# Expert choice in six parts spread over the blocks, and a bank map of its own for the last block

## The reference

```python
x = x + linear_attn(layernorm(x))        # 16 heads of 32, phi = elu + 1, causal running sums
# expert layer on the new x, 8 experts:
probs = softmax(layernorm(x) @ gate_w.T) # [16384, 8]
top2_w, top2_idx = top_k(probs, 2)       # ties go to the lower index
counts = bincount(top2_idx, length=8)
keep = counts <= int(1.25 * 16384 / 8)   # 2560: an expert with more tokens is dropped whole
out = x + sum over the two chosen experts of w * keep * ffn_e(layernorm(x))
```

## Time and profile before

| | us |
|---|---|
| median of 3 runs (2035.15 to 2038.97) | 2037.31 |
| profiled execution | 2035.86 |
| its span, first to last instruction | 2033.8 |
| PE busy in the span | 1972.9 (97%) |
| DVE busy | 1510.8 (74%) |
| POOL busy | 902.3 (44%) |
| ACT busy | 736.0 (36%) |
| load of 128 rows for the residual, issue to landing | 2.7 |
| store of them | 2.0 |

### The profile page before, as it was taken

One profiled execution on the slowest core, in us unless ns is written; L12 is line 12 of the kernel. 1 busy time (PEld: TensorE's weight loads), 2 busy tenths in 40 slices (PEclk: granted clock), 3 DMA queues, 4 the chain that ended last, 5 costly groups with the idle time before them and its releaser, 6 DMA issues.

```text
span 2033.8 us, 60809 instructions
## 1 busy us (share of the span) xinstructions
PE 1972.9 (97%) x25924; PEld 1736.7 (85%) x25924; DVE 1510.8 (74%) x3181; ACT 736.0 (36%) x1415; POOL 902.3 (44%) x987
## 2 busy tenths in 40 slices
PE   6899999999999999999999999999999999999985
PEld 5788888888888888888888888888888888888874
DVE  5677777777777777777777777777777777777767
ACT  3333343333343333343333333333343333333321
POOL 3454534554533554533554533554533554543521
PEclk8999999999999999999999999999999999999997
DMA  5221222221222221222221222221222221222110
GB/s 176 72 86 43 89 90 74 95 85 50 83 90 74 95 85 49 88 86 74 95 85 52 82 89 74 95 85 53 85 85 74 95 85 54 84 84 74 54 33 32
DMA packets 87388, 159.26 MB, mean 78 GB/s; under 512 B 15312, under 2 KB 15312, under 8 KB 87120
## 3 DMA queue, kind: packets, MB, share of 16 engines
q1 hardware_dynamic: 84720, 154.83, 22.5%
q10 hardware_dynamic: 2400, 0.55, 0.1%
HBM read 121.66 MB, written 33.68 MB: 76 GB/s over the span
## 4 chain that ended last, share of the span: by engine, by line
PE 91%; DVE 6%; POOL 1%; issue 1%; ACT 1%; DMA 0%; SPq 0%; POOLq 0%; DVEq 0%
PE ring L585 35%; PE ring L599 33%; PE num_ps L685 6%; PE ring L650 6%; PE num_ps L673 3%; PE ring L661 3%; PE num_ps L697 2%; DVE s_mask L847 2%; DVE den L1067 1%; PE ring L622 1%; PE ring L635 1%; DVE rden L1074 1%; DVE v_tok L877 1%; DVE o_lo L1063 1%; ACT o_hi L816 0%
## 5 line engine op out<-in xcount | busy, mean ns | idle before, releaser
L1136 POOL TENSOR_TENSOR k_sum<-k_sum,q_raw 128x512 f32<-128x512 f32 x128 | 164.6, 1286 | 588.8 <-DVE q_raw L858 588.8
L765 ACT ACTIVATE e_tmp<-ring,bias_n 128x512 f32<-128x512 f32 x256 | 176.0, 687 | 402.1 <-PE ring L585 402.1
L847 DVE TENSOR_TENSOR s_mask<-ring,causal 128x512 f32<-128x512 f32 x512 | 315.0, 678 | 0.0
L599 PE MATMUL ring<-wv_hi,xt_hi 128*128 128x260 f32 x1024 | 301.8, 295 | 3.1 <-DVE gate_x L879 2.3
L599 PE MATMUL ring<-wo_hi,o_hi 128*128 128x260 f32 x1024 | 290.7, 284 | 4.3 <-DVE o_lo L1063 3.5
L599 PE MATMUL ring<-wo_hi,o_lo 128*128 128x260 f32 x1024 | 293.0, 286 | 0.0
L599 PE MATMUL ring<-wo_lo,o_hi 128*128 128x260 f32 x1024 | 291.3, 284 | 0.0
L599 PE MATMUL ring<-wv_hi,xt_lo 128*128 128x260 f32 x1024 | 290.1, 283 | 0.0
L599 PE MATMUL ring<-wv_lo,xt_hi 128*128 128x260 f32 x1024 | 289.7, 283 | 0.0
L858 DVE SCALAR_TENSOR_TENSOR k_t<-ring,bias,e_tmp 128x512 f32<-128x512 f32 x128 | 96.1, 751 | 211.9 <-ACT e_tmp L767 209.0
L585 PE MATMUL ring<-xt_hi,wk_hi 128*128 128x512 f32 x512 | 215.3, 421 | 6.9 <-DVE wk_lo L310 5.6
(11 more groups left out here) (140 smaller groups left out, 4195.0 us busy)
## 6 DMA issues: line engine op xcount, KB each, us to landing
x_tok<-in_x SPq DMA_DIRECT2D x128, 256.0 KB, 3.7
res<-in_x SPq DMA_DIRECT2D x128, 256.0 KB, 2.7
out<-res SPq DMA_DIRECT2D x128, 256.0 KB, 2.0
x_in<-in_x_t SPq DMA_DIRECT2D x124, 256.0 KB, 4.5
x_rows<-moments_rows SPq DMA_DIRECT2D x31, 512.0 KB, 3.7
k_t<-in_wk_t SPq DMA_DIRECT2D x1, 1024.0 KB, 9.1
q_raw<-in_wq_t SPq DMA_DIRECT2D x1, 1024.0 KB, 11.3
v_tok<-in_wv_t SPq DMA_DIRECT2D x1, 1024.0 KB, 13.4
```

The source lines that it names most:

```text
L599: mm = pe.matmul(bank[:, 0:HW], rows[a](k), w[b][:, k, h, :], start=n == 0, stop=n == 3 * KD - 1)
L765: act.activation(e_tmp[:, m], bank, ACT.Relu, bias=bias_n[:, m, g:g + 1], scale=-1.0).then_inc(phi_relu.handle, 1)
L847: dve.tensor_tensor(s_mask[:, j], ring[:, BANK[u]].rearrange("p (g t) -> p g t", g=KD), repeat(causal, KD), ALU.mult).then_inc(free[BANK[u ...
L1136: pool.tensor_tensor(k_sum[:, g], k_sum[:, g], q_raw[:, g], ALU.mult).then_inc(prod.handle, 1)
```

## The change

1. `PARTS` has six parts instead of two: blocks 0-7, 8-15, 16-23, 24-28, 29-30 and 31, with 256, 256, 256, 160, 64 and 32 elements a partition. Parts 0 to 3 run within steady blocks (the last within block 30): steps 0 and 1 at the end of tile 3 of one block, and in the next block the exponential on ACT after `k_tok` of tile 0, steps 2 to 5 ahead of DVE's second projection chunks in tile 0, 6 to 12 at the end of tile 0, 13 to 16 in tile 1 and 17 to 18 in tile 2 ahead of `o_lo`. Part 4 is spread over the four tiles of block 31; its last two steps follow the last logits; part 5 comes at the end.
2. The steps work in place in two buffers, `den` and `rden_high` (which the denominators use in tile 2); ACT waits for the part to be over before it writes `den`. One step goes (product and sum are one `scalar_tensor_tensor`), and the count stands ahead of the weights: 19 steps.
3. Block 31 has a map of its own, `BANK_ALONE`: scores j in bank j, T in bank 4, O in banks 5 (first half) and 4 (second half). T(c+1) no longer shares a bank with scores.
4. The logits of block 31 go from POOL to DVE (`last_logits`), but for the power, which stays on POOL (`last_rstd`) with the copies of the moments.
5. PE sums the counts with six matmuls, one a part, each after its own part's count.

```diff
+BANK_ALONE = {**{("S", (c, j)): j for c in range(1, TPB) for j in range(HPG)},
+              **{("T", c): HPG for c in range(TPB)},
+              **{("O", (c, h)): HPG + 1 - h for c in range(TPB) for h in range(2)}}
...
+    def alone(self):
+
+        return self.parts == ("attn",)
+
+    def bank(self, u):
+
+        return BANK_ALONE[u] if self.alone() else BANK[u]
...
-CHOOSE_STEPS, SHIFTED = 20, 2
+CHOOSE_STEPS, SHIFTED, Z_LINKS = 19, 2, 6
...
-    half = KD * BT // 2
-    scratch = [buf.rearrange("p k t -> p (k t)")[:, h * half:(h + 1) * half] for buf in (x_in, k_sum)
-               for h in range(2)]
-    top_scratch = e_tmp[:, 0]
-    assert n_blocks * TPB * E <= half and n_blocks * TPB <= BT
-    PARTS = [(0, (n_blocks - 1) * TPB), ((n_blocks - 1) * TPB, n_blocks * TPB)]
+    z_rstd, z_last = sem("z_rstd"), sem("z_last")
+    scratch = (den, rden_high.bitcast(F32))
+    PARTS = [(0, 8), (8, 16), (16, 24), (24, n_blocks - 3), (n_blocks - 3, n_blocks - 1), (n_blocks - 1, n_blocks)]
+
+    def part_begun(t):
+
+        return [m for m, (a, b) in enumerate(PARTS[:4]) if b == t]
 
     def exponential(act, m):
         a, b = PARTS[m]
         act.wait_ge(chosen.handle, m * CHOOSE_STEPS + SHIFTED)
-        act.activation(z_all[:, a:b], z_all[:, a:b], ACT.Exp).then_inc(exp_done.handle, 1)
+        act.activation(z_all[:, a * TPB:b * TPB], z_all[:, a * TPB:b * TPB], ACT.Exp).then_inc(exp_done.handle, 1)
...
-                n = st.freed(u) if c else st.before(BANK[u]) + CREDIT
-                pe.wait_ge(free[BANK[u]].handle, n)
+                if c:
+                    pe.wait_ge(free[st.bank(u)].handle, st.freed(u))
+                else:
+                    pe.wait_ge(free[BANK[u]].handle, st.before(BANK[u]) + CREDIT)
...
-        pe.wait_ge(chosen.handle, chosen.at(2 * CHOOSE_STEPS))
-        for m in range(2):
-            mm = pe.matmul(ring[:, 0, 0:E], ones, count[:, m], start=m == 0, stop=m == 1)
+        for m in range(len(PARTS)):
+            pe.wait_ge(chosen.handle, chosen.at((m + 1) * CHOOSE_STEPS - 1))
+            mm = pe.matmul(ring[:, 0, 0:E], ones, count[:, m], start=m == 0, stop=m == len(PARTS) - 1)
...
+                if c == 0 and proj:
+                    for m in part_begun(st.off - 1):
+                        exponential(act, m)
...
-                if c == 0 and not proj:
-                    exponential(act, 0)
+                if c == 1 and st.alone():
+                    exponential(act, 4)
...
+                    for m in part_begun(st.off - 1):
+                        act.wait_ge(chosen.handle, (m + 1) * CHOOSE_STEPS)
...
-        exponential(act, 1)
+        exponential(act, 5)
...
+                if m < 5:
+                    dve.wait_ge(z_done.handle, z_done.at(PARTS[m][1]))
+                else:
+                    dve.wait_ge(z_last.handle, 1)
...
-                dve.tensor_scalar(left, picked, -2.0, None, ALU.mult).then_inc(chosen.handle, 1)
+                dve.scalar_tensor_tensor(key, picked, -2.0, z, ALU.mult, ALU.add).then_inc(chosen.handle, 1)
...
+        def last_logits(st):
+
+            b = st.off % 2
+            tiles = st.lin(TPB, st.off)
+            dve.wait_ge(gx_done.handle, gx_done.at(st.lin(1, st.off, 1)))
+            dve.wait_ge(x1_aggr.handle, x1_aggr.at(st.lin(TPB, st.off, TPB)))
+            dve.tensor_scalar(var1, mv1[:, :, 1], LN_EPS, None, ALU.add).then_inc(z_link.handle, 1)
+            dve.tensor_tensor(z_b, repeat(g_sum, TPB), over(mv1[:, :, 0:1], E), ALU.mult).then_inc(z_link.handle, 1)
+            dve.wait_ge(z_link.handle, z_link.at(st.lin(Z_LINKS, st.off, 2)))
+            dve.tensor_tensor(z_b, gate_x[:, b], z_b, ALU.subtract).then_inc(z_link.handle, 1)
+            dve.wait_ge(z_link.handle, z_link.at(st.lin(Z_LINKS, st.off, 3)))
+            dve.tensor_tensor(z_b, z_b, gate_o, ALU.add).then_inc(z_link.handle, 1)
+            dve.wait_ge(z_link.handle, z_link.at(st.lin(Z_LINKS, st.off, 4)))
+            dve.wait_ge(z_rstd.handle, 1)
+            dve.tensor_tensor(z_all[:, bass.ds(tiles, TPB), :], z_b, over(rstd1, E), ALU.mult).then_inc(z_last.handle, 1)
+            choose(4, range(17, CHOOSE_STEPS))
...
-                if c == 0 and not proj:
-                    dve.wait_ge(z_done.handle, z_done.at(st.lin(1, st.off)))
-                    choose(0, range(SHIFTED))
+                if c == 2 and proj:
+                    for m in part_begun(st.off - 1):
+                        choose(m, range(17, CHOOSE_STEPS))
...
+                if c < 2 and proj:
+                    for m in part_begun(st.off - 1):
+                        choose(m, range(2, 6) if c == 0 else range(13, 17))
...
-                    if not last:
-                        choose(0, range(SHIFTED + 5 * c, SHIFTED + 5 * c + 3))
-                    else:
-                        choose(0, range(SHIFTED + 5 * c, SHIFTED + 5 * c + 1))
+                if st.alone() and last:
+                    choose(4, range(13, 17))
                 if attn:
                     residual(st, c)
                     if c != 2 or not proj:
                         residual_moments(st, c)
-                if not proj:
-                    choose(0, range(SHIFTED + 5 * c + 1 + 2 * (not last), SHIFTED + 5 * c + 3 + 2 * (not last)))
+                if c == 0 and proj:
+                    for m in part_begun(st.off - 1):
+                        choose(m, range(6, 13))
+                if last and proj:
+                    for m in part_begun(st.off):
+                        choose(m, range(0, 2))
+                if st.alone() and not last:
+                    choose(4, (range(0, 2), range(2, 8), range(8, 13))[c])
+            if st.alone():
+                last_logits(st)
...
-        dve.wait_ge(z_done.handle, z_done.at(n_blocks))
-        choose(1, range(CHOOSE_STEPS))
+        choose(5, range(CHOOSE_STEPS))
...
+        def last_rstd(st):
+
+            pool.wait_ge(z_link.handle, z_link.at(st.lin(Z_LINKS, st.off, 1)))
+            pool.tensor_tensor(rstd1, var1, neg_half, ALU.pow).then_inc(z_rstd.handle, 1)
+            pool.wait_ge(z_rstd.handle, 1)
+            keep_moments(st)
...
-                if last and attn:
+                if last and attn and proj:
                     logits(st)
+                if last and st.alone():
+                    last_rstd(st)
```

More of the change, by code:

```diff
@@ L127, in use @@
     def use(self, u):
-        k = BANK[u]
-        rank = sum(BANK[v] == k for v in uses_of(self.parts)[:uses_of(self.parts).index(u)])
+        k = self.bank(u)
+        rank = sum(self.bank(v) == k for v in uses_of(self.parts)[:uses_of(self.parts).index(u)])
         n = self.base[k] + rank
@@ L237, in attention @@
     order = sb("order", [P, E])
[L238 removed]
+    count = sb("count", [P, 6, E])
+    top_prob = sb("top_prob", [P, 8 * TPB])
     z_a = sb("z_a", [P, TPB, E])
@@ L528, in store @@
             u = ("O", (c, 1))
-            sp.wait_ge(free[BANK[u]].handle, st.freed(u))
+            sp.wait_ge(free[st.bank(u)].handle, st.freed(u))
             sp.sem_inc(waited[sp.engine].handle, 1)
@@ L579, in project @@
             w = w_q if kind == "Q" else w_k
-            pe.wait_ge(free[BANK[u]].handle, st.claimed(u))
-            bank = ring[:, BANK[u]]
+            pe.wait_ge(free[st.bank(u)].handle, st.claimed(u))
+            bank = ring[:, st.bank(u)]
             n = 0
@@ L587, in project @@
                     n += 1
-            mm.then_inc(full[BANK[u]].handle, 1)
+            mm.then_inc(full[st.bank(u)].handle, 1)
         def two_halves(st, kind, c, rows, w):
@@ L692, in add_state @@
                 return
-            pe.wait_ge(free[BANK[("T", c)]].handle, st.freed(("T", c)))
+            pe.wait_ge(free[st.bank(("T", c))].handle, st.freed(("T", c)))
             for g in range(KD):
@@ L755, in relu_exp @@
             u, m = (kind, g), kind == "K"
-            act.wait_ge(full[BANK[u]].handle, st.filled(u))
-            bank = ring[:, BANK[u]]
+            act.wait_ge(full[st.bank(u)].handle, st.filled(u))
+            bank = ring[:, st.bank(u)]
             if g:
@@ L802, in body @@
                     u = ("T", c)
-                    act.wait_ge(full[BANK[u]].handle, st.filled(u))
-                    act.activation(k_tok, ring[:, BANK[u]], ACT.Copy).then_inc(free[BANK[u]].handle, 1)
+                    act.wait_ge(full[st.bank(u)].handle, st.filled(u))
+                    act.activation(k_tok, ring[:, st.bank(u)], ACT.Copy).then_inc(free[st.bank(u)].handle, 1)
+                if c == 0 and proj:
+                    for m in part_begun(st.off - 1):
+                        exponential(act, m)
                 if last and turns:
@@ L818, in body @@
                     u = ("DEN", 0)
-                    act.wait_ge(full[BANK[u]].handle, st.filled(u))
-                    act.activation(den, ring[:, BANK[u], 0:BT // 2], ACT.Copy,
-                                   bias=DEN_EPS).then_inc(free[BANK[u]].handle, 1)
```

(13 more changed lines are left out.)

89 lines of the change are left out of this document (45 added, 44 removed).

## The result

The changed kernel takes 2014.05 us (median of 4 runs, 2012.44 to 2015.74), the kernel before 2037.57 (4 runs, 2035.15 to 2038.97). The ratio is 0.9886 with a 95% interval of 0.9869 to 0.9903: 23.5 us less. The forecast was 2014.

A forecast was written before the change was run, and what follows sets the result against it. PE's own work bounds the steady part, its waits the stretch from block 31 on. Gains 20.7 (block 31) + 1.6 (tail) + 0.4 (links) + 0.4 (count) = 23.1 us; forecast 2014, range 2011 to 2017.5.

The forecast's parts named there:

- Steady blocks: Blocks before 31: the added choice steps fit DVE's slack and cost PE 0 us, with 0 to 3 us kept.
- collisions with POOL: DVE steps with two SBUF inputs and POOL instructions hold each other up by 0.6 to 0.8 us.
- Cost of a step: DVE steps of the choice: 0.45 us for 256 elements, 0.36 for 160, 0.26 for 64.
- Block 31: Last block: `o_lo` of tile 0 earlier, tiles about 7.5 us apart, last moments end at 2000.23; gain 20.7 us.
- s(0): Start of `o_lo` of tile 0 in block 31: 1972.19, where before it was 1977.49.
- The tail: From the last moments to the last part's first step: 2.3 us instead of 3.93, gain 1.6.
- the prediction's other case: Tail: POOL's power pays the slow first instruction (0.98 us instead of 0.23), so the gain there is 0.9.
- (a): Rival, chance 0.14: PE's clock falls in block 31; 2016 if only the last projection falls, 2021.6 if all tiles.
- (b): Rival, chance 0.08: steady blocks lose 0.7 to 1.3 us a part to POOL collisions and used-up DVE slack; 2017 to 2019.
- (d): Rival, chance 0.03: slower than before, port collisions in blocks 9, 17, 25, 30 cost some 7 us a block; 2042.
- (c): Rival, chance 0.05: in block 31 the hold moves to `keep_state` and `k_tok` between O's halves; 2017.
- (e): Rival, chance 0.02: the new bank map ties T to another late reader, holds stay; within 2 us of before.

The follow-up runs named there:

- `k_tok` first: Changed kernel with ACT copying the next tile's turned keys (`k_tok`) ahead of `keep_state` in block 31 only; 2010.61 us, ratio 0.9866 to the kernel before.

## Why the prediction was right

**What bounds the kernel.** Confirmed. PE's own work sets the steady part, and adding 24 us of DVE work between 200 and 1800 us moved it by less than its scatter. The whole gain lies behind T(0).

**Steady blocks, taken at 0, kept 0 to 3.** Right: no more than 0.1 us a block. The size of the slack ahead of Q3's `phi` was about right, 1.2 said and 0.9 measured. What the prediction didn't see is that the next tight places, the masks and K's `phi`, are not far behind. The collisions with POOL were foreseen from two rows of before. They are real, two in each part of 256 elements, of 0.78 and 0.4 us, at two of eleven steps with two SBUF inputs (the prediction counted ten). The Trainium skill, "SBUF — State Buffer", section "Who interferes with whom", states that a DVE instruction with two SBUF inputs contends with a GpSimd instruction that reads SBUF, and calls the ports they share an exclusive lock. Beside POOL's additions the trace agrees, where the step ends 0.28 us after POOL's instruction; beside POOL's power on four elements it doesn't, where the step took its usual 0.42. The cost here falls on DVE's slack only. The Trainium skill, "VectorE: DVE Perf Modes", section on the TRN2 errata, speaks against small tiles for their fixed cost; the trace agrees on that cost (0.19 us for 32 elements, 24 us more of DVE in 200 to 1800), but it cost no time, as DVE isn't the bound there.

**Cost of a step.** Right. A step took 0.42 us for 256 elements, 0.22 to 0.23 for 64 and 0.19 for 32, and from one start to the next it was 0.46, 0.25 and 0.22, where the prediction, gap included, had 0.45, 0.26 and 0.22: the line through two rows of before held.

**Block 31.** s(0) came 3.61 us after T(0), 3.62 forecast; the tiles 7.43, 7.60 and 7.36 us apart, where 7.58, 7.68 and 7.43 were given. In the first, DVE's two steps ahead of the exponential took 0.45 us for 0.52 and the exponential 0.26 for 0.3. The last projection, 3.05 to the last residual by the prediction, took 3.17 (1999.15 to 2002.32). O's second half started 2.91 us after `o_lo` in tile 0 (1978.92), where 2.98 was given; the prediction's own addends, 0.92, 1.30, 0.60 and 0.14, give 2.96. Moments' end minus T(0) is 31.47 us against 52.33 before, a gain of 20.86 where 20.7 was given.

**The tail.** 2.02 us where 2.3 was said, a gain of 1.9 for 1.6; the power took 1.02 as counted, POOL began it 0.08 after the variance instead of 0.18, and product and two steps took 0.55 together instead of 0.72. So one size was off, DVE's side put 0.3 too high. The 3.93 us before that it was taken from hold POOL's slow first instruction (0.98), which the kernel with the map alone shows too; the prediction's other case, that the power pays it, didn't come. Of the 1.9 us 1.2 are the place of the logits and 0.7 that this instruction is no longer slow, which the run with POOL's logits shows without moving them. The links (0.45 for 0.4) and the count (0.49 for 0.4) were right.

**The total.** 23.1 forecast, 23.7 from T(0) to the end, 23.5 between the medians. The two agree this well partly by luck: the profiled execution had a fast last projection (as six of seven with this code; a slow one would give 22.4), and the start of an execution wanders by 5 us.

**Rivals.** (a) was given 0.14 as a thing that holds or doesn't. It is neither: the small form of it, the last projection alone, comes in some executions and not in others, at 1.3 to 1.5 us where 1.7 was said. The large form, all tiles slow, wasn't seen. (b) and (d) are ruled out by the lengths of blocks 9, 17, 25 and 30 with and without steps and the unchanged list of waits, (c) by the 0.44 us ahead of O's second half, where the prediction's own sum had 0.8 us, (e) by T(1) starting without a wait.

## What to carry to other kernels

Where a hold on the last block has two causes in a row (a bank tied to a late reader, and a queue filled with long steps), take both away: one alone brought 3.8 us, the other 14.8, both 23.7. Work that must be done anyway can be cut into parts and laid under a bound engine at no cost as long as each part fits the other engine's slack, and doubling it shows how near the edge is: here one part fits a block and two don't. Compare stretches between two marks in the traces when the start of an execution scatters by more than the effect, and take them as short as one block: that showed a cost of 0.9 us a block of which the list of waits had 0.3. Holds on PE also cost clock: a quarter of what their removal gave was faster matmuls.

## What the runs showed of the hardware that was not expected

The same program, with the same 1.9 us of idle time on PE ahead of its last projection, keeps the granted clock in one execution and falls to its lower level in the middle of the projection in another (matmuls 0.12 us apart, then 0.22): it fell in one execution of seven with the changed kernel's code there and in three of three with `k_tok` first.

Identical code up to block 0's first `q_div` ended between 126.98 and 132.19 us. In the chain of the changed kernel's first profile the first load of x took 6.20 us, where it took 5.25 before and 5.32 in its second; and between 70 and 100 us its granted clock was 0.89, against 1.00 in the second, in which one group of 24 projection matmuls took 5.68 us instead of 7.67. What decides either was not tried.

POOL's first instruction of the last logits, on 128x4 elements, took 0.98 us in both executions with the old choice (after 13.77 and 15.04 us of idle time) and 0.31 in the run with POOL's logits (7.59 us), where it takes 0.23 in the other blocks. Idle time alone doesn't do it: another POOL instruction of this size (`std<-var,mv`) took 0.20 after 16.54 us of it. What decides it was not tried.
